# Queries and keys projected by features, and their high and low parts sent to the score stacks by direct DMA

## The reference

```python
x_norm = _ln(x) * (1 + scale) + shift
q, k, v = jnp.split(x_norm @ qkv_W, 3, axis=-1)      # 16 heads of 16 features
q, k = _apply_rope(q, cos, sin), _apply_rope(k, cos, sin)   # layers 0 and 3
s = jnp.einsum('bqhd,bkhd->bhqk', q, k) / 4
a = jax.nn.softmax(jnp.where(mask, s, lowest), axis=-1)
x = x + gate * (jnp.einsum('bhqk,bkhd->bqhd', a, v) @ out_W)
```

## Time and profile before

| | |
|---|---|
| median of 3 runs | 3388.25 us (3383.53 to 3397.24) |
| profiled execution | 3385.59 us, its span 3383.8 us |
| mean granted TensorE clock | 0.983 of 2.4 GHz |
| PE busy | 3198.4 us, 95% |
| weight loads busy (beside PE) | 2208.4 us, 65% |
| DVE busy | 2039.6 us, 60% |
| ACT busy | 1715.7 us, 51% |
| DMA on SP's queue | 101.02 MB, 13.1% of 16 engines |

### The profile page before, as it was taken

The page is one execution under the profiler, slowest core; times in us unless marked ns, Lnnn a source line. Parts: engine busy times, 40 slices in busy tenths (PEclk is TensorE's granted clock), DMA queues, the critical chain, the costliest instruction groups (busy, mean ns, idle before and its releaser), DMA issues.

```text
span 3383.8 us, 61434 instructions
## 1 busy us (share of the span) xinstructions
PE 3198.4 (95%) x23165; PEld 2208.4 (65%) x23230; DVE 2039.6 (60%) x5184; ACT 1715.7 (51%) x2739; POOL 291.3 (9%) x340
## 2 busy tenths in 40 slices
PE   5999999999999999997999999999999999999998
PEld 4556666666666766665666666676666666676676
DVE  2665556656665466676566656665666766666662
ACT  0445454454445455543555556556545465555564
POOL 0001000000000111101110111111000000000000
PEclk9999999999999999998999999999999999999999
DMA  4011011111011222211111111111121110101100
GB/s 147 19 20 25 18 26 24 24 22 30 21 26 21 79 66 47 46 33 40 25 26 22 28 24 22 28 23 37 20 59 20 18 22 18 22 22 20 20 15 15
DMA packets 103077, 104.95 MB, mean 31 GB/s; under 512 B 13881, under 2 KB 98553, under 8 KB 102538
## 3 DMA queue, kind: packets, MB, share of 16 engines
q1 hardware_dynamic: 102794, 101.02, 13.1%
HBM read 54.75 MB, written 16.86 MB: 21 GB/s over the span
## 4 chain that ended last, share of the span: by engine, by line
PE 41%; DVE 5%; ACT 3%; issue 3%; DMA 1%; SPq 0%; POOL 0%; ACTq 0%; DVEq 0%; POOLq 0%
PE gen L862 10%; PE gen L1045 6%; PE gen L1036 5%; PE gen L994 5%; PE gen L914 4%; DVE row_max L1356 2%; PE score L969 2%; PE score L931 2%; PE score L944 2%; PE gen L1005 1%; ACT probs L1138 1%; DMA q_stack<-maxT 1%; PE gen L871 1%; PE score L975 1%; PE gen L1016 1%
## 5 line engine op out<-in xcount | busy, mean ns | idle before, releaser
L1356 DVE TENSOR_REDUCE row_max<-score 128x4 f32<-128x1024 f32 (+1 forms) x640 | 651.2, 1049 | 219.2 <-PE score L931 135.1
L1138 ACT ACTIVATE probs<-score 128x1024 f32<-128x1024 f32 (+1 forms) x576 | 571.1, 1027 | 359.0 <-PE score L969 279.5
L1122 ACT CAST q_stack<-gen 128x512 fp32r<-128x512 f32 x448 | 256.7, 600 | 239.7 <-PE gen L914 238.5
L1036 PE MATMUL gen<-xnT,w_w 128*128 128x256 f32 x1536 | 368.9, 386 | 4.9 <-ACT xnT L1092 4.4
L1045 PE MATMUL gen<-w_w,hT 128*128 128x256 f32 x1536 | 354.0, 384 | 4.7 <-ACT hT L1160 3.7
L1170 POOL TENSOR_TENSOR rstd<-var_eps,minus_half 128x2 f32<-128x2 f32 x160 | 112.8, 705 | 2776.8 <-DVE var_eps L1211 2776.6
L1045 PEld LDWEIGHTS gen<-w_w,hT 128*128 128x128 f32 x1536 | 286.6, 191 | 53.1 <-issue 13.6
L1036 PEld LDWEIGHTS gen<-xnT,w_w 128*128 128x128 f32 x1536 | 280.5, 190 | 54.0 <-issue 10.6
L862 PE MATMUL gen<-w_qkv,xnT 128*128 128x512 f32 (+1 forms) x768 | 285.6, 505 | 6.8 <-ACT xnT L1092 6.4
L914 PE MATMUL gen<-ident,q_tok 128*128 128x128 f32 x1792 | 261.2, 278 | 15.5 <-DVE k_tok L1331 7.9
L1160 ACT ACTIVATE hT<-gen,b_b 128x256 f32<-128x256 f32 x384 | 160.5, 472 | 222.8 <-PE gen L1036 221.8
(11 more groups left out here) (139 smaller groups left out, 4898.8 us busy)
## 6 DMA issues: line engine op xcount, KB each, us to landing
q_stack<-maxT SPq DMA_DIRECT2D x448, 64.0 KB, 2.4
x_scratch<-x SPq DMA_DIRECT2D x48, 256.0 KB, 2.2
x_in<-x_scratch SPq DMA_DIRECT2D x48, 256.0 KB, 2.8
gate<-gates_scratch SPq DMA_DIRECT2D x80, 128.0 KB, 3.2
w_w<-in_L_w SPq DMA_DIRECT2D x6, 1024.0 KB, 7.7
ctx_in<-in_ctx SPq DMA_DIRECT2D x64, 77.0 KB
x_in<-in_x SPq DMA_DIRECT2D x16, 256.0 KB, 3.5
out_x<-x SPq DMA_DIRECT2D x16, 256.0 KB, 2.1
```

The lines of the kernel that those rows point to most:

```text
L1036: mm = pe.matmul(buf[:, i * S:i * S + S], w["w1"][:, fc, col:col + P], xnT[s][:, fc, :], start=fc == 0, stop=fc == FC - 1)
L1122: act.copy(q_stack[s][:, 2 * j:2 * j + 2, :], src).then_inc(gen_moved[st.fill.buf], 1)
L1138: act.activation(probs[st.probs][0:keys, :, :], score[st.fill.buf][0:keys, :, :].rearrange("p a (r q) -> p (a r) q", r=2), ACT.Exp, bias=k ...
L1356: dve.tensor_reduce(dst, src, AX_X, ALU.max).then_inc(max_done[b], 1)
```

## The change

Queries and keys are projected with features on partitions: the weights stand still, `xnT` (or `ctxT`) moves, and the bank holds two chunks of 128 features by 256 tokens (77 for the context). A rotation then works on whole tiles with a shuffle of partitions (`rt`, DVE), ACT writes the high part (`hi`) and DVE the low part (`lo`) of all heads into one buffer `parts`. SP places them (`pl`): for each of three row groups and each of four groups of 32 partitions one DMA from `parts` to every fourth partition of the stack, and for queries one more that puts zeros on the rows of the maxima: 13 for queries, 12 for keys. The context's values get a projection and a copy of their own. The maxima go with one DMA for a half instead of two; their rows are now every fourth partition. PE's `stack` steps, ACT's `eQ` and `eK`, and DVE's `split` are gone. The plan counts 0.45 us of SP for each DMA issued, and SP's steps are chosen by rank as on the other engines. Before the jobs start, tables, zeros and the rows of ones are made and placed once.

```diff
+ISSUE = 0.45
...
+    if name == "rt":
+        return 1.45 if context else 2.75
...
+    if name == "pl":
+        return 7.2 if context else 7.8
...
-            split = qkv = None
-            for j in range(TC):
-                qkv = add("qkv", j, "pe", [xe, ready, qkv])
-                split = add("split", j, "dve", [add("rot", j, "dve", [qkv, split], qkv)])
...
-            for j in range(PAIRS // 2):
-                for name, moved in (("Q", q_moved), ("K", k_moved)):
-                    stk = add("stk" + name, j, "pe", [split])
-                    moved[j] = add("e" + name, j, "act", [stk], stk)
+        def high_and_low(j, fill):
+            value = add("rt", j, "dve", [fill], fill) if blk.rope else None
+            high = add("hi", j, "act", [value or fill])
+            low = add("lo", j, "dve", [high], None if blk.rope else fill)
+            return add("pl", j, "sp", [low])
+            qkv = add("qkv", 0, "pe", [xe, ready])
+            queries = high_and_low(0, qkv)
+            qkv = add("qkv", 1, "pe", [xe, ready, qkv])
+            keys = high_and_low(1, qkv)
...
-            rows = add("S", u, "pe", [q_moved[u // 2 if blk.whole else u], k_moved[u // 2]])
+            rows = add("S", u, "pe", [queries, keys])
...
-                st = min(can, key=lambda st: (st.job, 0) if eng == "sp" else (7 * st.job - st.rank, 0))
+                st = min(can, key=lambda st: (8 * st.job - st.rank, 0))
...
-                if eng != "sp":
-                    busy[eng] = now + took
-                    events.append((now + took, None))
+                busy[eng] = now + (took if eng != "sp" else ISSUE * issues(st))
+                events.append((busy[eng], None))
...
+                def place_parts(st):
...
+                    sp.wait_ge(*lo_finished(of(st, "lo", st.j)))
+                    if way(st) == 0:
+                        none = zeros_dram.unsqueeze(1).to_broadcast([1, n_pairs, n])[0].partition_broadcast(4 * PAIRS)
+                        sp.dma_start(rows[0:P:4], none).then_inc(parts_placed[0][s], 16)
+                    for part, low in enumerate((0, 0, 1) if way(st) == 0 else (0, 1, 0)):
+                        for i in range(n_pairs):
+                            src = source[4 * PAIRS * i:4 * PAIRS * (i + 1), low, 0:n]
+                            sp.dma_start(rows[1 + part:P:4, i, :], src).then_inc(parts_placed[way(st)][s], 16)
...
-                    if blk.whole and j < TC:
-                        mm = project(buf[:, :], xnT[s][:, :, j * P:j * P + P], w["qkv"], slice(0, 2 * D))
-                    elif context:
-                        mm = project(buf[0:CTX, :], ctxT[s], w["ckv"], slice(0, 2 * D))
+                    if j < 2:
+                        weight, at_col = (w["qkv"], j * D) if blk.whole else (w["ckv"], 0) if context else (w["cq"], 0)
+                        xT, out = ctxT[s] if context else xnT[s], by_chunk(st, buf)
+                        for c in range(FC):
+                            cols = slice(at_col + c * P, at_col + c * P + P)
+                            for fc in range(FC):
+                                mm = pe.matmul(out[:, c, :], weight[:, fc, cols], xT[:, fc, :], start=fc == 0, stop=fc == FC - 1)
...
-                    pe.wait_ge(*moved(of(st, "stkQ", u // 2 if blk.whole else u)))
-                    pe.wait_ge(*moved(of(st, "stkK", u // 2)))
+                    pe.wait_ge(*placed(of(st, "pl", 0)))
+                    pe.wait_ge(*placed(of(st, "pl", 1)))
```

More of the change, by code:

```diff
@@ L314, in run @@
     def run(self):
-        rings = {"gen": GEN, "score": SCORES, "back": BACKS, "qtok": 1, "ktok": 1, "hid": 1, "wide": WIDE, "own": OWN,
+        rings = {"gen": GEN, "score": SCORES, "back": BACKS, "hid": 1, "parts": PARTS, "turned": TURNED, "own": OWN,
                  "max": MAXIMA, "x_in": X_IN, "ctx_in": CTX_IN}
@@ L319, in run @@
         owner, issued, halves = None, 0, []
-        busy = {eng: 0.0 for eng in ENGINES}
+        busy, loads = {eng: 0.0 for eng in ENGINES}, {"ldx": 0, "ldc": 0}
         could = {eng: [] for eng in ENGINES}
@@ L339, in part @@
         def part(st, ring):
-            j = {"max": st.j, "back": st.j, "wide": st.j}.get(ring, 0)
+            j = {"max": st.j, "back": st.j, "parts": st.j, "turned": st.j}.get(ring, 0)
             return ring, st.job, st.k, j
@@ L351, in startable @@
                 return False
-            if "wide" in st.takes and len(empty["wide"]) == 1 and part(st, "qtok") not in held:
+            if st.name in loads and loads[st.name] != st.job:
                 return False
@@ L666, in dit_stack @@
         pause = sb("pause", [P, 1])
-        rope_b = bias["qkv"][:, 0:2 * D].rearrange("p (h d) -> p h d", d=HD)
-        wide = [sb(f"wide{i}", [P, 2 * H, HD]) for i in range(WIDE)]
+        turned = [sb(f"turned{i}", [P, FC * S]) for i in range(TURNED)]
         hT = sb("hT", [P, FFC, S])
@@ L899, in project_in @@
[L899 to L914 removed]
+                            mm = project(buf[:, c * D:c * D + D], xnT[s][:, :, c * P:c * P + P], w["qkv"], slice(2 * D, 3 * D))
```

418 lines of the change are left out of this document (214 added, 204 removed).

## The result

| | before | after |
|---|---|---|
| median of 4 runs each, same chip | 3392.74 us (3383.53 to 3399.32) | 3663.82 us (3647.26 to 3668.37) |
| ratio to before, 95% interval | | 1.0795 (1.0768 to 1.0822) |
| span of the profiled execution | 3383.8 us | 3658.7 us |
| PE busy / idle | 3198.4 / 185.4 us | 3144.6 / 514.1 us |
| granted TensorE clock | 0.983 | 0.881 |

The account below looks back on a forecast made before the run. PE was taken to bound the kernel, busy 95% of the span. 3385.6 - 346 (transposes) + 15 (start) + 11 (layer 1) + 67 (waits) = 3133 us, as a median 3135 us, -7.5%; range 3050 to 3340 us.

Parts of the forecast that it names:

- PE time that goes is worth nearly its full price: PE, whole kernel: removing 346 us of transposes saves nearly that much, if stacks arrive in time.
- C: Rival: less PE work does not come back as time, gaps widen, clock falls, half the gain goes; 3239 us, 8%.
- PE gets 0: PE's projections of queries, keys and context values: reshaped records cost no extra time; upper end +63 us.
- ACT and DVE: Both engines get lighter (ACT loses about 440 us, gets about 160); both waited for PE, so counted 0.
- An issue costs 0.50 us: SP's DMA issues: 0.50 us each, bounds 0.37 and 0.61, so SP issues for 1650 us, half the span.
- A placement takes 8 to 9 us: Stack placements by SP: 6.0 us to issue twelve DMAs plus 2.4 us landing; transposes and copies took 3 to 4.
- Rival B: Transfers replace transposes, slower: PE waits at first scores and score columns, 1 us for each of 448; 3560 us, 11%.
- The rule on issuing: Skill page: initiating a DMA is usually small; trace disagreed; by the rule, time about 10 us less.
- Start +15 us: Kernel start: 74 DMAs ahead of the first maxima end at 136 us; +15 us, bounds +5 and +24.
- Layer 1, 17.1 us a job: Layer 1: PE needs 16.4 us a job, SP 14.8; taken 17.1, +11 us for 16 jobs, bounds 0 and +48.
- The rest, 0.15 us for each of 448 transfers: PE's waits for 224 placements and 224 maxima transfers: +67 us, bounds -24 and +448.
- The clock stays in my sum: Granted TensorE clock, whole run: no loss counted, bound +100 us.

Follow-up runs that it names:

- e2: Changed kernel with three DMAs for a placement in place of twelve, same bytes but other values, order unchanged: 3234.16 us, ratio 0.9542.
- e17: Kernel before with 2176 of 3072 transposes left out and half of each copy, order as before: 3336.24 us, ratio 0.9835.
- e15: Kernel before with 1728 of 3072 transposes left out, copies and order kept: 3374.54 us, ratio 0.9944.
- e1: Changed kernel with measured issue, placement and maxima costs told to the plan, only the order differing: 3538.88 us, ratio 1.0433.
- e6: Changed kernel with parts stored to memory and loaded back in few DMAs, plan told costs measured in e4: 3259.19 us, ratio 0.961.
- e13: Changed kernel with the planner's weight of the job number at 7 in place of 8: 3706.14 us, ratio 1.0922.
- e14: e1 with the planner's weight of the job number at 7 in place of 8: 3519.73 us, ratio 1.0371.
- e4: Changed kernel with parts stored to memory and loaded back, plan told 3.0 us store, 5.6 and 4.8 us loads: 3325.86 us, ratio 0.981.
- e3: e2's three DMAs, with the plan told of them (placements 5.6 and 4.9 us): 3379.42 us, ratio 0.9964.
- e8: Kernel before with 48 DMAs of other forms added at its end, to read issue costs; one execution, 0.63 to 0.66 us each in a row, one load form 0.49.
- e7: e1 with the twelve DMAs of each key placement issued by ACT instead of SP: 3682.89 us, ratio 1.0846.
- e9: Kernel before with the planner's weight of the job number at 8 in place of 7: 3532.59 us, ratio 1.0423.

## Why the prediction was wrong, point by point

The prediction added 93 us of waits (15 + 11 + 67) and nothing for dearer work. The profile has 329 us more idle time and 292 us of dearer work. These 236 and 292 us are what lies between the forecast and the measured time. Two terms hold them: the waits that SP's issues make, taken at 0.15 us a transfer, and the clock, taken at 0. With three quarters of the issues gone (e2) 430 of the 529 us are gone too; e2 still lies 99 us above the forecast and above the forecast's own range of 3060 to 3210 us; the first step below is about that rest.

- **"PE time that goes is worth nearly its full price."** This step failed too, and no DMA is needed to show it: e17 takes 190 us from PE and gets 58, 30%; e15 takes 145 and gets 19; e2, with few issues on SP, gets 159 of 346, 46%. What is lost in e17 is idle time (83 us) and dearer work (49 us). The prediction had this as C, with 8%, but let PE's 98% in layer 0 argue against it. The 59% of DVE is no measure of the slack of a chain in fixed order: a mean share says how much an engine has to do, not when.
- **PE gets 0.** Right. Eight records of 77 columns take 1.01 us (0.126 each, taken 0.105, bound 0.228), and the projections of queries and keys kept their price.
- **ACT and DVE.** Right in size: ACT is busy for 224 us less (the prediction's figures give 280), DVE for 184 (228). The shuffle of partitions, in no row before, takes 734 ns, one 512-wide pass, as taken (DVE group by shape: busy us, mean ns):

```profile
L1340 DVE STREAM_SHUFFLE parts<-gen 128x512 f32<-128x512 f32 x80 | 58.8, 734 | 0.8 <-issue 0.4
```

- **An issue costs 0.50 us, bounds 0.37 and 0.61.** Mis-sized, and outside the bounds: the instruction takes 0.594 us as the maxima's did, but twelve in a row stand 0.635 us apart (7.62 us). SP issues for 2800 x 0.635 + 224 x 0.64 + 306 x 0.37 = 2035 us (2043 us by the trace), 56% of the span, not 1650. I took the value between two rows where the row of the same kind of transfer was at hand.
- **A placement takes 8 to 9 us.** By the medians of the trace it takes 8.8 to 9.1 us for keys and 10.2 us for queries, so this term was nearly right; the plan had 7.2 and 7.8. Rival B named just this, "a plan that reckons with 0.45 us and lands 12 DMAs later than planned": another order, made with costs near these, was worth 125 us in e1. The overlap of landings was right (2.1 us each), so the time is far below the 6700 us of the rule of single transfers.
- **The rule on issuing.** The prediction set the page "DMA: Bandwidth & Descriptors" of the Trainium skill (Issuing engines are not separate DMA queues), by which initiating is usually small beside the DMA, against 0.6 us for 64 KB. The runs side with the trace, and much more so than the 10 us given to it: a quarter of the issues with the same bytes is worth 430 us. The other rule of this page of the Trainium skill (Rules for kernel authors), to join small transfers into a large one, was dismissed for its mechanism; its advice was right here, by e2 and by e6, for the issues' sake and not for the landing's.
- **Start +15 us.** Right, by luck: the first maxima are issued at 133.4 us, before at 116.2 us, +17. But the first parts were issued at 86.6 us and not near 96.4, and the 74 issues took 47 us, not 37; the two errors cancel.
- **Layer 1, 17.1 us a job.** Two jobs end 17.5 us apart each (stores at 1514.92 and 1549.99), near in such a stretch. But over the whole layer nothing is gained: from the 16th to the 32nd store of x pass 378 us, before 376 us. That is 23.5 us a job already before, so the 19.1 us that the prediction read from two jobs were the pace of a calm stretch and not of the layer. In e2 they take 285 us. The step reckoned an SP busy for 87 to 90% as if it cost only its own rest.
- **The rest, 0.15 us for each of 448 transfers, +67 us.** Failed by size: PE waits for these transfers 214 us by name and up to 69 us more under "issue". The waits are few and up to 14 us, since a batch of issues stands ahead of another job's maxima on SP. A mean of 0.15 us over transfers, read where SP issued for 12% of the span (411 us), said nothing about an SP that issues for 56% of it in blocks of twelve.
- **"The clock stays in my sum."** Failed by size: taken at 0 with a bound of +100 us, measured +292. Behind a wait of 4.76 us eight records take 3.52 us, 2.00 us elsewhere.
- **The DMA engines' load.** Forecast some 37%, measured 28.0%. At the price it names, 13.1% for 101 MB, the 272 MB would be 35%. Nothing hangs on it: this load was not the trouble, as e6 moves more and is faster.

What the prediction gave as its tests came out against it: PE busy 3145 us, not 2850 to 2900; clock 0.881; PE at 86% of the span, below 88%. The waits for q_stack and the keys lie, with those under "issue", at 283 us, just under the 300 us that B was to need, and B's sum is short of the measured time by 104 us. B's mechanism, waits behind blocks of issues, is shown; C's comes on top, where the prediction had them as alternatives.

Not settled: why the weight 8 costs the old stacks 4%, beyond that it makes many small gaps and a lower clock; how much of each distance between two of these kernels is the luck of an order, since one weight alone moved it by up to 139 us; and what beside idle time lowers the clock where the transposes are gone. A filler that keeps PE busy in its waits, which would measure the clock's part by itself, was not tried; the split into idle and clock is read from the profiles, not from an experiment.

## What to carry to other kernels

A busy share near 100% on one engine tells what bounds the kernel, not what its time is worth once it is taken away: look for the chains that are only just covered, and do not count on the full price; here 13% to 46% of it came back. Work that is thinned out of a block saves less than the block's pace says (0.2 us were left where 0.114 us were reckoned). Before moving work to DMAs count the issues, at the pace of issues in a row and on the engine that makes them; few large transfers by a detour can beat many direct ones (3259 against 3664 us here). In a kernel whose order is planned ahead, a single weight moved the time by up to 4%, over half of what the change was to gain: measure new costs, tell them to the plan, and time more than one order. In four pairs here (after and e1, e13 and e14, e4 and e6, e3 and e2) the order made with placements told too short was the slower, by 67 to 186 us.

## What the runs showed of the hardware that was not expected

- The pace of issues in a row on SP: 0.63 us for what reads SBUF, with 64 KB from 32 partitions as with 256 KB from 128; 0.49 us for loads from memory to 128 partitions and 0.66 us for those to every fourth partition with four rows each (e8); a single store takes 0.37 us. A 256 KB DMA from SBUF to 32 partitions with four rows each takes longer to issue: 0.99 us in e8 (four in 3.95 us), 0.86 us (queries) and 1.28 us (self keys) in the mean in e2.
- 256 KB from 32 partitions to every fourth partition land after 4.8 to 5.4 us, 64 KB after 2.1 us; from memory the same 256 KB land after 4.3 to 4.7 us.
- Twelve issues on ACT's queue held ACT's own work for 8.7 us (e7, at 1517.28 us).
- The granted clock of the whole run was lower where idle time of PE grew, with no DMA and no work added: 0.967 in e17 and 0.952 in e9, for 0.983.
- A transpose of 128x128 costs 0.114 us of PE in a row of 32 and 0.213 us in the mean where it stands alone (e17).
